# A message-passing layer and a mixture of experts on one core: the gather of pair j+2 ahead of the scatter of pair j-1 on GpSimd

## The chip, the core and the metric

The kernel runs on one core of one Trainium2 chip. The metric is the device time of one execution in microseconds (us); a program on one core has the time of that core. Before the change, three runs took 1000.0, 990.54 and 1000.09 us, with a median of 1000.0.

## What is computed

The input is 1250 rows of 512 floats and 20000 edges. Two layers follow each other, each added to its input:

```python
x = x + gnn(layernorm(x), edge_index, edge_type, edge_weight, ...)   # attention over edges, then a layer norm
x = x + ffn(layernorm(x), ...)                                        # 64 experts, two per row, and a shared one

# ffn, for T = 1250 rows, E = 64 experts, D = 512, H = 256
scores = sigmoid(xt @ Wg.T + bg)
w, idx = top_k(scores, 2);  w = w / w.sum(-1)
nx = layernorm(xt)
h = silu((gamma[e] * nx + beta[e]) @ W1[e] + b1[e]) * (... @ W3[e] + b3[e])   # per expert e
y = sum over the two experts of w * (h @ W2[e]) + cw @ b2
z = shared expert on nx (Ws1, Ws3, Ws2)
return y + z
```

All is float32. W1 and W3 are 512 x 256 for each expert and W2 is 256 x 512, so two experts have 2 MB of W1 and W3 and 1 MB of W2.

## The kernel before

The edge layer comes first and takes until about 490 us; then come its layer norm, the router and the table of slots, and from about 597 us the experts. The change touches the experts only.

**Pairs of experts.** The experts are taken in 32 pairs (`NPAIR`), pair j being experts 2j and 2j+1, each with up to 64 rows (`TS`). `slot_tab` holds, for each pair, the 128 row numbers to read (column 0) and the 128 places to write (column 1); places that no row fills carry a number out of bounds and are skipped. What does not fit into 64 rows goes through a loop behind the pairs, which ran once here.

**The steps of one pair, by line.** All buffers between these steps have two copies, taken by j % 2.
- GpSimd gathers 128 rows of `nx_rows` (DRAM) into `xg` (line 538), which raises `xg_landed[j % 2]`.
- TensorE turns `xg` by four transposes (`turn`, lines 982 to 985, recorded as L762) and raises `pe_xgT`; VectorE scales the result (lines 1514 and 1515) and raises `xgT_done`.
- TensorE multiplies by W1 and W3 (`up`, the bias as L989, the rest as L993; raises `pe_up`). ScalarE takes the silu (L718), VectorE multiplies (L1522) and raises `hm_done`.
- TensorE turns the hidden rows (`hidden_turn`, again L762); VectorE copies them (L1525) and raises `hT_done`.
- TensorE multiplies by W2 (`down`, L1006; raises `pe_y`). ScalarE copies the 128 rows to `yo` (L721) and raises `y_ready`.
- GpSimd scatters `yo` into `y_rows` in DRAM (L543), which raises `y_out[j % 2]`.

**Order on TensorE** (lines 1013 to 1046): in iteration j it does up(j), then waits for the gather of pair j+1 (line 1022) and does turn(j+1), then down(j-1), then work on the side, then hidden_turn(j). The work on the side is the shared expert and the turned router weights in iterations 0 to 6 (`BESIDE`, L927 and L933) and one product of the biases in each of iterations 7 to 16 (L1041).

**Order on GpSimd** (lines 550 to 557): the gathers of pairs 0 and 1 ahead of the loop; then in iteration j it waits for turn(j), gathers pair j+2, waits for the output rows of pair j and scatters them. GpSimd takes its instructions one by one, so a wait holds all that stand behind it. Pair 32 is the first item of the loop behind the pairs.

**Loads of the weights.** There are three buffers (`WB`). SP issues W1 and W3 of pair j+3 when up(j) is done (lines 397 to 399, L372). ScalarE issues W2 of pair j+2 after down(j-1) (line 734, L714), but behind a wait for an earlier scatter:

```python
act.wait_ge(s("pe_y"), j)
if j >= 3:
    act.wait_ge(y_out[(j - 1) % 2], 16 * ((j - 1) // 2))   # the scatter of pair j-3 has landed
if j - 1 + WB < NPAIR:
    load_down(j - 1 + WB)
out_rows((j - 1) % 2, P, "y_ready")
```

Of the kernel before, what the change touches and what calls it, by code (L numbers as in the profile page):

```python
# [38 lines left out]
def gnn_moe_kernel(nc, x, src, dst, etype, eweight, W, a_src, a_dst, et_emb, ln_gamma, ln_beta,  # L39
# [23 lines left out]
    REST = NE - FULLC * P  # L63

    NEX, _, HF = W1.shape
    M = HF // P
    TS = TOKENS
    NOV = (2 * N) // TS
    NPAIR = NEX // 2
# [23 lines left out]
    with ExitStack() as ctx:  # L93
# [4 lines left out]
        def sem(name):  # L98
            return ctx.enter_context(nc.semaphore(name))
# [190 lines left out]
        def s(name):  # L290

            if name not in names:
                names[name] = sem(name)
            return names[name]
# [4 lines left out]
        y_out = [sem(f"y_out{k}") for k in range(2)]  # L299
# [126 lines left out]
        def _(pool):  # L426
# [110 lines left out]
            def gather(u, at, sems):  # L537
                pool.indirect_dma_start(out=xg[:, u, :], out_offset=None, in_=nx_d[:, :],
                                        in_offset=bass.IndirectOffsetOnAxis(ap=at, axis=0),
                                        bounds_check=NPAD - 1, oob_is_err=False).then_inc(sems, 16)  # L540

            def scatter(u, at, sems):
                pool.indirect_dma_start(out=y_d[:, :], out_offset=bass.IndirectOffsetOnAxis(ap=at, axis=0),  # L543
                                        in_=yo[:, u, :], in_offset=None, bounds_check=2 * NPAD - 1,
                                        oob_is_err=False).then_inc(sems, 16)

            def slots(j, k):
                return slot_tab[:, j:j + 1, k:k + 1].rearrange("p a b -> p (a b)").bitcast(U32)

            gather(0, slots(0, 0), xg_landed[0])  # L550
            gather(1, slots(1, 0), xg_landed[1])
            for j in range(NPAIR):
                if j + 2 <= NPAIR:
                    pool.wait_ge(s("pe_xgT"), j + 1)
                    gather(j % 2, slots(j + 2, 0), xg_landed[j % 2])
                pool.wait_ge(s("y_ready"), j + 1)
                scatter(j % 2, slots(j, 1), y_out[j % 2])
            pool.wait_ge(y_out[0], 16 * (NPAIR // 2))
            pool.wait_ge(y_out[1], 16 * (NPAIR // 2))
            n = pool.value_load(nover_i[0:1, 0:1], min_val=0, max_val=NOV)  # L560
# [1048 lines left out]
```

## Time and profile before

| What | Value |
|---|---|
| median of three runs | 1000.0 us (990.54 to 1000.09) |
| the profiled execution's own time | 996.03 us |
| its span, first to last instruction | 994.3 us |
| busy: TensorE, VectorE, ScalarE, GpSimd | 719.7, 546.5, 276.1, 385.8 us |
| mean granted TensorE clock | 0.836 of full speed |
| bytes moved, mean rate over the span | 190.72 MB, 192 GB/s |

The span and the rows come from one execution; the granted clock of 1.00 is 2.4 GHz and that of 0.50 is 1.2 GHz; 1.7 us of its time lie outside its span. PE is TensorE's matrix work and PEld its loading of weights into the array, which runs beside it; DVE is VectorE, ACT ScalarE, POOL GpSimd, and SPq and ACTq are the instructions by which SP and ScalarE issue transfers. "DMA share" is the mean busy share of the core's 16 DMA engines. A row of the timeline that stands for several instructions (x4) gives the time from the first one's start to the last one's end. A number in square brackets at the end of such a row is the time for which the engine sat idle before it, and what ended that.

### The profile page before, as it was taken

The page shows a single profiled execution, that of the slowest core. Times are in us where ns is not written, and L with a number is a line of the kernel's source. Part 1 is how long each engine was busy: PE and PEld are TensorE (multiplying, and loading weights), DVE is VectorE, ACT ScalarE, POOL GpSimd, SP SyncE. Part 2 cuts the span into 40 slices and gives each one's busy share as a digit, 9 for nine tenths or more (in the row PEclk, how much of TensorE's full clock was granted, in tenths as well). Part 3 has the DMA queues.
Part 4 walks back from the last instruction along what each step waited for, and adds up shares of the span by engine and source line. Part 5 has one row for each costly group of instructions (what it writes and reads, how often), then busy time and mean ns, then how long its engine had stood idle before and what let it go on. Part 6 is the DMA issues. An engine that isn't in the chain of part 4 may idle for free.

```text
span 994.3 us, 12428 instructions
## 1 busy us (share of the span) xinstructions
PE 719.7 (72%) x3500; PEld 375.2 (38%) x3500; DVE 546.5 (55%) x1238; ACT 276.1 (28%) x735; POOL 385.8 (39%) x397
## 2 busy tenths in 40 slices
PE   0979885156987797776607999898787877777740
PEld 0966563133544344443306554333232222222210
DVE  4978999844876576667897584223232221221205
ACT  0344441157254655455026310110001000010000
POOL 2415543976277777778353011112111121122110
PEclk9777988577998889978755799999999898898885
DMA  5323435376168656855132006889889788888228
GB/s 176 88 58 100 106 97 160 89 215 181 48 173 268 209 165 178 295 165 141 68 122 84 23 15 233 295 307 362 303 304 330 295 309 291 309 330 299 97 76 309
DMA packets 67755, 190.72 MB, mean 192 GB/s; under 512 B 15420, under 2 KB 16625, under 8 KB 67712
## 3 DMA queue, kind: packets, MB, share of 16 engines
q1 hardware_dynamic: 37172, 99.66, 28.9%
q0 software_dynamic: 19440, 56.41, 18.7%
q10 hardware_dynamic: 11100, 34.11, 9.8%
q8 instruction: 24, 0.39, 0.2%
q14 instruction: 19, 0.16, 0.0%
HBM read 180.78 MB, written 16.57 MB: 198 GB/s over the span
## 4 chain that ended last, share of the span: by engine, by line
PE 43%; DVE 17%; DMA 16%; issue 12%; another core or an unknown queue 3%; POOL 3%; ACT 2%; DVEq 1%; ACTq 1%; POOLq 0%; SPq 0%
PE ps L877 14%; DMA xn<-nx_rows,slot_tab 12%; PE ps L1006 8%; PE ps L762 5%; DVE edge L1210 3%; PE ps L880 3%; POOL y_rows L543 3%; DVE arena L1203 2%; PE ps L927 2%; PE ps L993 2%; PE ps L821 2%; ACT xn L721 2%; DMA ring<-y_rows 2%; PE ps L841 1%
## 5 line engine op out<-in xcount | busy, mean ns | idle before, releaser
L877 PE MATMUL ps<-ring,edge 128*128 128x512 f32 x320 | 180.5, 692 | 66.5 <-DVE ring L1286 35.0
L489 POOL DMA_INDIRECT ring<-h_rows,idx_stage x160 | 171.9, 1074 | 42.9 <-issue 38.8
L635 ACT ACTIVATE ring<-ring,edge 128x64 f32<-128x64 f32 x480 | 128.6, 336 | 115.3 <-DMA ring<-h_rows,idx_stage 101.0
L543 POOL DMA_INDIRECT y_rows<-xn,slot_tab x32 | 33.5, 1047 | 280.7 <-ACT xn L721 268.2
L762 PE MATMUL ps<-ident,xn 128*128 128x128 f32 x278 | 62.9, 355 | 98.0 <-DMA xn<-nx_rows,slot_tab 60.8
L1282 DVE TENSOR_SCALAR edge<-iota_row,dloc 128x128 f32<-128x128 f32 x176 | 61.2, 348 | 89.8 <-remote 57.8
L877 PEld LDWEIGHTS ps<-ring,edge 128*128 128x128 f32 x320 | 61.9, 216 | 114.5 <-issue 64.8
L762 PEld LDWEIGHTS ps<-ident,xn 128*128 128x128 f32 x278 | 46.8, 212 | 152.8 <-DMA xn<-nx_rows,slot_tab 85.5
L1522 DVE TENSOR_TENSOR xn<-ps,xn 128x256 f32<-128x256 f32 (+1 forms) x33 | 14.0, 425 | 148.5 <-ACT xn L718 81.1
L993 PE MATMUL ps<-arena,xn 128*64 128x512 f32 x352 | 80.8, 601 | 0.0
L1006 PE MATMUL ps<-arena,xn 128*64 128x512 f32 x260 | 78.6, 727 | 0.9 <-DVE xn L1525 0.9
L1286 DVE TENSOR_TENSOR ring<-ring,edge 128x320 f32<-128x320 f32 x160 | 77.6, 485 | 0.0
L880 PEld LDWEIGHTS ps<-edge 128*128 128x128 f32 x352 | 58.2, 207 | 48.6 <-issue 48.6
L457 POOL TENSOR_SCALAR arena<-arena 24x1280 bf16<-24x1280 bf16 (+1 forms) x11 | 37.9, 3450 | 80.3 <-DMA arena<-edge_keys 80.3
L721 ACT COPY xn<-ps 128x512 f32<-128x512 f32 (+1 forms) x33 | 19.3, 585 | 164.5 <-PE ps L1006 164.5
L466 POOL TENSOR_TENSOR spare<-iota_p 128x1 f32<-128x1 f32 x63 | 21.0, 334 | 105.4 <-DVE slot_tab L1483 54.4
L1274 DVE TENSOR_TENSOR acc<-ps,acc 128x512 f32 x88 | 60.6, 688 | 0.4 <-issue 0.4
L718 ACT ACTIVATE xn<-ps 128x256 f32<-128x256 f32 (+1 forms) x33 | 12.6, 383 | 168.9 <-PE ps L993 168.9
L1210 DVE TENSOR_REDUCE edge<-arena 128x40 f32<-128x800 f32 (+1 forms) x32 | 50.4, 1576 | 4.8 <-DVE arena L1203 4.6
L880 PE MATMUL ps<-edge 128*128 (+1 forms) x352 | 47.9, 245 | 0.0
L993 PEld LDWEIGHTS ps<-arena,xn 128*64 128x64 f32 x352 | 23.4, 137 | 56.4 <-issue 56.4
L821 PE MATMUL ps<-arena,xT 128*128 128x512 f32 x80 | 43.7, 697 | 0.0
(284 smaller groups left out, 1046.5 us busy)
## 6 DMA issues: line engine op xcount, KB each, us to landing
arena<-in_L_ffn_W_dram SPq DMA_DIRECT2D x47, 1024.0 KB, 10.8
arena<-in_L_ffn_W_dram ACTq DMA_DIRECT2D x29, 1024.0 KB, 5.4
edge<-in_L_ffn_W_dram SPq DMA_DIRECT2D x20, 1024.0 KB
arena<-edge_keys SPq DMA_DIRECT2D x20, 320.0 KB
ring<-y_rows SPq DMA_DIRECT2D x9, 512.0 KB, 6.3
ring<-edge_keys SPq DMA_DIRECT2D x10, 320.0 KB
h_rows<-ring SPq DMA_DIRECT2D x10, 256.0 KB, 4.5
ring<-h_rows,idx_stage POOLq DMA_INDIRECT x160
```

Of the source, the lines that this page charges most:

```text
L489: pool.indirect_dma_start(out=(ring2 if lo == 1 else ring)[:, slot, :], out_offset=None, in_=h_d[:, :], in_offset=bass.IndirectOffsetOnAxi ...
L543: pool.indirect_dma_start(out=y_d[:, :], out_offset=bass.IndirectOffsetOnAxis(ap=at, axis=0), in_=yo[:, u, :], in_offset=None, bounds_chec ...
L635: o = act.activation(rows[:, k, h * HD:(h + 1) * HD], rows[:, k, h * HD:(h + 1) * HD], ACT.Copy, scale=p_c[:, bass.ds(SLOTS * i + k, 1), h ...
L762: return pe.transpose(o, i, ident[0:n, 0:n])
L821: o = pe.matmul(ps[:, 7, :], xT[:, a, t * P:(t + 1) * P], WT[:, a, :], start=(a == 0), stop=(a == A - 1))
L877: pe.matmul(ps[:, j % 4, :], S[:, k % 4, :], rows[:, k, :], start=(u == 0), stop=(u == 1))
L880: o = pe.matmul(ps[:, 4 + j % 4, 0:H], S[:, k % 4, :], p_c[:, bass.ds(SLOTS * i + k, 1), :].rearrange("p a h -> p (a h)"), start=(u == 0), ...
L993: o = pe.matmul(ps[c, 2 + k, :], xgT[:, k, a, c], w13[b][:, x, :, a, :], start=False, stop=(a == A - 1), skip_group_check=True)
L1006: o = pe.matmul(ps[c, 5 + k, :], hT[:, k, m, c], w2s[b][:, x, m, :], start=(m == 0), stop=(m == M - 1))
L1210: link(v.tensor_reduce(e_c[:, c0:c0 + n, :], prod[:, 0:n * 2 * NT * H].rearrange("p (c k h) -> p c h k", c=n, h=H), AX_X, ALU.add))
L1282: v.tensor_scalar(S[:, k % 4, :], iota_row[:, :], dloc[:, bass.ds(SLOTS * i + k, 1)], None, ALU.is_equal)
L1286: v.tensor_tensor(rows[:, k, 0:n].rearrange("p (h d) -> p h d", d=HD), rows[:, k, 0:n].rearrange("p (h d) -> p h d", d=HD), p_c[:, bass.ds ...
```

## The change

The loop on GpSimd gets one more iteration, and in iteration j the scatter is that of pair j-1 instead of pair j. The gather keeps its place at the head of the iteration and its wait.

```diff
-            for j in range(NPAIR):
+            for j in range(NPAIR + 1):
                 if j + 2 <= NPAIR:
                     pool.wait_ge(s("pe_xgT"), j + 1)
                     gather(j % 2, slots(j + 2, 0), xg_landed[j % 2])
-                pool.wait_ge(s("y_ready"), j + 1)
-                scatter(j % 2, slots(j, 1), y_out[j % 2])
+                if j >= 1:
+                    pool.wait_ge(s("y_ready"), j)
+                    scatter((j - 1) % 2, slots(j - 1, 1), y_out[(j - 1) % 2])
```

Written out, with G for a gather and S for a scatter, the queue of GpSimd was G0 G1 G2 S0 G3 S1 G4 S2 ... G32 S30 S31 and becomes G0 G1 G2 G3 S0 G4 S1 G5 S2 ... G32 S29 S30 S31. The count of instructions, their sizes and all semaphores stay the same.

## Rows read from the trace of the kernel before

**Rows 1.** The page, the chain that ended last: shares by line.
```profile
PE ps L877 14%; DMA xn<-nx_rows,slot_tab 12%; PE ps L1006 8%; PE ps L762 5%; DVE edge L1210 3%; PE ps L880 3%; POOL y_rows L543 3%; DVE arena L1203 2%; PE ps L927 2%; PE ps L993 2%; PE ps L821 2%; ACT xn L721 2%; DMA ring<-y_rows 2%; PE ps L841 1%
```
**Rows 2.** Waits, 600 to 994 us: engine, line, releaser: us, times, longest.
```profile
POOL y_rows L543 <- ACT xn L721: 268.2, 31, 18.5
...
PE ps L762 <- DMA xn<-nx_rows,slot_tab: 60.8, 25, 4.1
...
PE ps L989 <- DMA arena<-in_L_ffn_W_dram: 3.3, 1, 3.3
```
**Rows 3.** Timeline, 819 to 835 us: start, us, engine, line, operation.
```profile
821.63 0.75 PE L762 MATMUL ps<-ident,xn 128*128 128x128 f32 x4 [2.42 <-DMA xn<-nx_rows,slot_tab]
...
822.32 1.94 PE L1006 MATMUL ps<-arena,xn 128*64 128x512 f32 x8
...
824.71 0.58 ACT L721 COPY xn<-ps 128x512 f32<-128x512 f32 x1 [5.06 <-PE ps L1006]
...
825.48 3.65 PE L993 MATMUL ps<-arena,xn 128*64 128x512 f32 x16
...
826.10 1.03 POOL L543 DMA_INDIRECT y_rows<-xn,slot_tab  x1 [7.56 <-ACT xn L721]
...
827.43 1.01 POOL L538 DMA_INDIRECT xn<-nx_rows,slot_tab  x1 [0.30 <-issue]
...
829.17 1.01 SPq L372 DMA_DIRECT2D arena<-in_L_ffn_W_dram  x2
...
833.21 1.13 PE L762 MATMUL ps<-ident,xn 128*128 128x128 f32 x4 [4.07 <-DMA xn<-nx_rows,slot_tab]
...
834.26 3.68 PE L1006 MATMUL ps<-arena,xn 128*64 128x512 f32 x8
```
**Rows 4.** Timeline of PE alone: bias products of pairs 1, 7, 8, 31; three turns.
```profile
605.86 1.02 PE L989 MATMUL ps<-arena,xn 128*128 128x512 f32 x2
...
622.20 0.75 PE L762 MATMUL ps<-ident,xn 128*128 128x128 f32 x4 [0.87 <-DMA xn<-nx_rows,slot_tab]
...
632.44 0.75 PE L762 MATMUL ps<-ident,xn 128*128 128x128 f32 x4 [1.94 <-DMA xn<-nx_rows,slot_tab]
...
655.66 0.75 PE L762 MATMUL ps<-ident,xn 128*128 128x128 f32 x4 [1.39 <-DMA xn<-nx_rows,slot_tab]
...
672.82 1.02 PE L989 MATMUL ps<-arena,xn 128*128 128x512 f32 x2
...
681.29 1.02 PE L989 MATMUL ps<-arena,xn 128*128 128x512 f32 x2
...
938.54 1.02 PE L989 MATMUL ps<-arena,xn 128*128 128x512 f32 x2
```
**Rows 5.** Windows of 1 us, PE alone: length, busy, clock, DMA share, GB/s.
```profile
634.00:635.00 1.00, 1.00 (x6) 0.50 1.06 434
775.00:776.00 1.00, 1.00 (x8) 1.00 0.00 0
834.00:835.00 1.00, 1.00 (x4) 0.50 1.03 414
```
**Rows 6.** Longer windows: length, PE, PEld, DVE, ACT, POOL, clock, DMA share, GB/s.
```profile
680.00:690.00 10.00, 7.34 (x32) 2.88 (x32) 2.10 (x5) 0.97 (x2) 2.05 (x2) 1.00 1.01 403
...
780.00:790.00 10.00, 7.19 (x29) 2.65 (x29) 2.70 (x6) 0.44 (x2) 2.04 (x2) 0.85 1.02 404
...
870.00:880.00 10.00, 5.97 (x26) 2.33 (x24) 0.85 (x2) 0.97 (x2) 2.04 (x2) 0.95 1.00 367
```
**Rows 7.** Window 625 to 925 us, the same columns.
```profile
625.00:925.00 300.00, 241.23 (x914) 85.66 (x911) 74.09 (x149) 27.37 (x57) 55.20 (x54) 0.92 0.85 310
```
**Rows 8.** DMA, 600 to 994 us: GpSimd's queue: packets, MB, share; issues to landing.
```profile
q0 software_dynamic: 5120, 9.74, 7.0%
...
xn<-nx_rows,slot_tab POOLq DMA_INDIRECT x30, 4.5
...
y_rows<-xn,stage_s POOLq DMA_INDIRECT x1, 2.3
```
**Rows 9.** Timeline of PE: the first bias product behind the pairs.
```profile
953.73 2.08 PE L989 MATMUL ps<-arena,xn 128*128 128x512 f32 x2 [3.26 <-DMA arena<-in_L_ffn_W_dram]
```

## The prediction

> **What bounds the kernel now.** I read the chain first. Its second entry is the transfer that fetches rows for the experts, with 12% of the span [rows 1], which is 0.12 x 994.3 = 119 us and all of it behind 600 us. A chain share is not what would be saved, since it holds the whole flight of each gather, beside which TensorE partly works. So the view of waits comes next, for that stage: TensorE itself sat idle 60.8 us in 25 waits for the gather, and for weights in a single wait of 3.3 us [rows 2], which belongs to the loop behind the pairs [rows 9]. No pair waited for its weights. GpSimd meanwhile stood 268.2 us before its scatters [rows 2].
>
> The timeline shows why the gather is late [rows 3]. Turn, down, hidden turn and up run from 821.63 to 825.48 + 3.65 = 829.13 us. The output rows are copied at 824.71, the scatter goes out at 826.10, and only behind it, at 827.43, the gather for the next turn. It lands some 5 us later, so TensorE is idle for 4.07 us, until 833.21. The two buffers of `xg` had long allowed that gather: turn of the pair before ended at 822.4. What held it was the wait for the output rows, one place ahead in GpSimd's queue.
>
> DMA is close to being the bound but isn't. Over 625 to 925 us its share was 0.85 at 310 GB/s [rows 7], and there are stretches in which nothing moved at all, such as 775 to 776 us with TensorE at work [rows 5]: all that had been asked for had landed, up to two pairs ahead.
>
> **What the change does, part by part.** Nothing is added: 33 gathers ahead of the extra loop and 32 scatters remain, near 1 us of GpSimd each [rows 3]. The gather of pair j+2 used to stand behind the scatter of pair j-1, which waits for down(j-1) in TensorE's iteration j. Now it stands behind the scatter of pair j-2, so it goes out in iteration j-1. Its own wait, for turn(j), is met in the same iteration ahead of down(j-2), so it adds no wait. The pattern on GpSimd (scatter, then gather, some 2.7 us behind the copy) stays as it is; the gather in it is merely the one for a pair later. Its lead over the need grows by one pair. It was 829.13 - 827.43 = 1.7 us; it becomes 1.7 us plus a cycle of at least 7.5 us, so at least 9.2 us. The median flight is 4.5 us [rows 8], the one of rows 3 took at most 5.8. So the 60.8 us of waits go, in the present queues. The scatters move past one gather each; that gather was issued an iteration earlier, and nothing waits in front of the scatter that did not before. The cost of this move I put at 0; were its cover gone, it would be one issue, 1.0 us [rows 3], of which ScalarE would feel nothing before a scatter were two pairs late.
>
> A second thing goes with the waits. After 4.07 us of idleness the granted clock is 0.50, the lower level of 1.2 GHz [rows 5]: down takes 3.68 us instead of 1.94 and turn 1.13 instead of 0.75 [rows 3]. That is 2.1 us per such wait.
>
> **What is late next.** TensorE without the waits, from the bias product of pair 1 at 605.86 us [rows 4]: up to pair 7 it stands at 672.82 now. The waits in that stretch are 0.87, 1.94 and 1.39 us, and the second was followed by the lower clock at 634 us [rows 5], 2.1 us: sum 6.3, so pair 7 comes at 666.5. From pair 7 to 17 each cycle has the bias product on the side, 681.29 - 672.82 = 8.47 us without a wait [rows 4], so 84.7 us. The last 14 cycles are 829.13 - 821.63 = 7.5 us each [rows 3], 105 us. Pair 31 could thus start at 666.5 + 84.7 + 105 = 856.2 us, where it starts at 938.54 now [rows 4]. TensorE alone would give 82.3 us.
>
> The weights don't allow all of it. A pair has 3 MB of weights, 3.146 MB in the decimal count. GpSimd's queue moved 9.74 MB in 64 transfers [rows 8], 0.30 MB for a gather and a scatter. So a pair is 3.45 MB. At 8.47 us that would be 407 GB/s, at 7.5 us 460 GB/s, and the fullest stretches of 10 us show 403, 404 and 367 [rows 6]. The rate when DMA never rests is not in this trace for long. The bounds: 404 GB/s, 8.54 us per pair, from above; from below the 310 GB/s at share 0.85, scaled to a full share, 365 GB/s or 9.45 us. The low estimate charges for the thin parts in which a gather or scatter runs alone and which would then lie beside weights. I take 385 GB/s, between them and near the mean 391 of the three full stretches: 9.0 us.
>
> W1 and W3 of pair j+3 are issued when up(j) ends. From the end of up(7), at 666.5 + 4.7 = 671.2 us, until those of pair 31 have landed are 22 pairs, from 10 to 31. 22 x 9.0 = 198 us, which gives 869 us. That is 13 us behind TensorE's own 856, so DMA ends last and the weights take the gather's place in the waits, from about the twentieth pair, once the lead of two pairs is used up. TensorE then idles about 1.5 us per cycle; waits of 2.0 and 2.4 us in this trace kept the full clock, as the one before 821.63 did [rows 3], so I charge nothing there.
>
> Pair 31 moves from 938.5 to 869: -69.5 us. What follows it is untouched: the last down, the loop behind the pairs and the stores wait for the same things. The profiled execution took 996.0 us, which gives 926.5. The median of the runs, 1000.0, lies 4 us over the profiled one, so the sum is put at 1000.0 - 69.5 = 930.5, and I say 931.
>
> The full stretches show 403 and 404 GB/s [rows 6]. The Trainium skill's page "DMA: Bandwidth & Descriptors", section "Where 436 GB/s comes from", says that for transfers between HBM and SBUF the memory side binds at about 358 GB/s for a core. The trace disagrees over 10 us, but not over 200, and the rule is a rival below.
>
> **The rivals.**
> - *The sustained rate is lower.* The queues can't hold what 10 us of them show: 345 to 365 GB/s, the scaled rate of rows 7 being its upper end. For it speaks that 870 to 880 us gave 367 at a full share [rows 6]. Against it, two of three full stretches gave over 400. At 358 GB/s a pair is 9.64 us, 22 of them 212 us, pair 31 starts at 883: -55 us, 945. With 345 it is 10.0 us, 220, 891: -47, 953. (By the skill's rule it would be just this 358 and 945.)
> - *TensorE stays the bound.* DMA holds 404 or more, pair 31 comes at 671.2 + 22 x 8.54 = 859 us or at TensorE's 856: -80 to -82, so 918 to 920. The idle 1 us at 775 [rows 5] speaks for slack; the 460 GB/s that 7.5 us would ask speaks against.
> - *The new waits cost clock.* If each wait for weights brought the lower level, a cycle would be 2.1 us longer: 856.2 + 24 x 2.1 = 907 us, -32, 968. The falls at present follow waits near 4 us, and a slower TensorE gives DMA time, which ends the waits. Weak.
> - *The gather stays late*, because with two of them ahead and full queues it flies longer than 9 us, or because its place depends on something that I misread: within 1% of before, 990 to 1010. The longest wait now is 4.1 us, so flights are near 6.
> - *Slower: the scatters land too late.* ScalarE waits for the scatter of pair j-3 ahead of the W2 load and of the copy. In a DMA queue that never empties a write to DRAM could take long. The place: that wait; the price: a cycle becomes (flight + 2.4 us from copy to issued scatter) / 2 [rows 3]. It is now (938.54 - 672.82) / 24 = 11.07 us [rows 4]. The time rises by over 1% only where the cycle passes 11.07 + 16/24 = 11.74, so with flights over 21 us. At 24 us the cycle is 13.2, +51 - 6: 1045. The one flight shown is 2.3 us [rows 8] with empty queues, gathers fly 4.5 in half full ones; 21 is far.
>
> **How the numbers follow.** My forecast (DMA ends last at 370 to 400 GB/s, 922 to 941) has 0.55, the lower rate 0.25, TensorE as the bound 0.10, the clock 0.04, the late gather 0.03, the scatters 0.03. The first three span 917 to 953; with the spread of the runs (990.5 to 1000.1) the range is 914 to 957, which leaves out about 0.15. A measurement of this kernel tells about 1% from no change. Faster by over 1%: all but the last two, 0.94. Within 1%: 0.03. Slower: 0.03.
>
> **What would show it.** In the profile after, the wait of TensorE's L762 for the gather should be near zero; waits of L989 or L993 for the weights (arena, edge) should appear in the last third; GpSimd should issue scatter and gather in the same pattern; the share of DMA from about 680 us on should be 0.97 or more, at 370 to 400 GB/s; pair 31's bias product should come near 869 us, with the cycles of pairs 8 to 16 at 8.5 us and the last ones at 9.0. If DMA's share stays under 0.9 with no gather wait left, my account of what is late next is wrong; if the gather wait is still there, that of the queue is.

## The result, and the profile after

The changed kernel took 928.96 us in the median of four runs (921.75 to 930.88), the one before 1000.05 us in four runs (990.54 to 1001.14). The ratio is 0.9295 with a 95% interval of 0.9219 to 0.9372: 7% faster. The prediction was 931 us. Executions more than 1.5% above the fastest of their kernel are left out of the ratios here, so that a ratio need not be the quotient of the two medians, and three of the profiled executions below (the release put back, W2 issued by SP, the last of the spread kernel) are of that kind.

The profiled execution took 930.39 us with a span of 928.6 us. The diff adds one line ahead of TensorE's code, so each line there is one higher: L763 is the turns (L762 before), L990 the first bias product of a pair (L989), L994 up, L1007 down.

The waits of TensorE behind 590 us, whole, to set against [rows 2] (engine, line, releaser: us, times, longest):

```profile
engine line waited for: us in total, times, longest us
PE ps L990 <- DMA arena<-in_L_ffn_W_dram: 10.6, 6, 3.5
PE ps L990 <- DMA edge<-in_L_ffn_W_dram: 2.7, 1, 2.7
PE ps L763 <- issue: 1.9, 1, 1.9
PE ps L763 <- DVE xn L1523: 0.9, 1, 0.9
PE ps L1007 <- DVE xn L1526: 0.9, 2, 0.5
PE ps L990 <- issue: 0.6, 1, 0.6
```

The 60.8 us of waits for the gather are gone to the last one. In their place stand 13.3 us of waits for weights, 3.5 of them in the loop behind the pairs. The page of the kernel after says the same of the chain: the gather's entry of 12% [rows 1] is missing and the weights have 7%.

```profile
PE ps L878 15%; PE ps L994 10%; DMA arena<-in_L_ffn_W_dram 7%; PE ps L763 5%; PE ps L1007 5%; PE ps L881 3%; DVE edge L1211 3%; PE ps L928 3%; PE ps L990 3%; DVE arena L1204 3%; PE ps L822 2%; PE ps L934 2%; DMA ring<-y_rows 2%; PE ps L798 2%
```

Where the time went is read best from the bias products, one per pair (timeline of TensorE; pairs 0, 7, 8, 17, 18, 20, 21, 22, 25, 29, 30 and 31; compare [rows 4]):

```profile
600.47 1.10 PE L990 MATMUL ps<-arena,xn 128*128 128x512 f32 x2 [0.59 <-issue]
...
670.25 1.02 PE L990 MATMUL ps<-arena,xn 128*128 128x512 f32 x2
678.52 1.02 PE L990 MATMUL ps<-arena,xn 128*128 128x512 f32 x2
...
752.98 1.02 PE L990 MATMUL ps<-arena,xn 128*128 128x512 f32 x2
760.41 1.02 PE L990 MATMUL ps<-arena,xn 128*128 128x512 f32 x2
...
775.26 1.02 PE L990 MATMUL ps<-arena,xn 128*128 128x512 f32 x2
785.57 1.48 PE L990 MATMUL ps<-arena,xn 128*128 128x512 f32 x2 [2.72 <-DMA arena<-in_L_ffn_W_dram]
794.75 1.02 PE L990 MATMUL ps<-arena,xn 128*128 128x512 f32 x2
...
820.58 2.08 PE L990 MATMUL ps<-arena,xn 128*128 128x512 f32 x2 [2.67 <-DMA arena<-in_L_ffn_W_dram]
...
855.67 1.13 PE L990 MATMUL ps<-arena,xn 128*128 128x512 f32 x2 [2.66 <-DMA edge<-in_L_ffn_W_dram]
863.95 1.12 PE L990 MATMUL ps<-arena,xn 128*128 128x512 f32 x2 [0.59 <-DMA arena<-in_L_ffn_W_dram]
871.53 1.13 PE L990 MATMUL ps<-arena,xn 128*128 128x512 f32 x2
```

From pair 7 to 17 each cycle is 8.27 us, then 7.43 us, without a wait, until pair 21. From there weights are late for six of the ten pairs 21 to 30. I call the time from the bias product of pair 0 to that of pair 31 the stage. It is 871.53 - 600.47 = 271.1 us, and was 938.54 - 596.98 = 341.6 us: 70.5 us less. Ahead of the stage this execution was 3.5 us later than the profiled one of before, and behind it 57.1 us against 55.8.

The windows (columns as in [rows 6]):

```profile
671.00:860.00 189.00, 179.83 (x741) 63.94 (x740) 57.53 (x121) 21.36 (x44) 45.02 (x44) 0.98 1.01 402
788.00:789.00 1.00, 1.00 (x6) 0.37 (x4) 0.00 (x0) 0.00 (x0) 0.00 (x0) 0.50 1.03 414
860.00:870.00 10.00, 9.41 (x42) 3.62 (x42) 3.15 (x8) 1.35 (x3) 2.05 (x2) 1.00 0.74 281
870.00:880.00 10.00, 9.49 (x42) 3.19 (x40) 2.36 (x5) 1.56 (x3) 1.65 (x2) 1.00 0.07 25
```

DMA moved 402 GB/s over these 189 us, where it had 310 at a share of 0.85 [rows 7]. Its share was still 0.81 from 670 to 680 us and full from there on (shares a little over 1 are read as full), with 408 GB/s from 700 to 860 us. It ran dry between 860 and 880 us, when the last weights were in. The second row is the lower clock behind the wait of 2.72 us.

### The profile page after: what moved, and what is told of

Same layout as the page of the kernel before. It is cut to its first block, busy times and chain, and to the rows that moved or that the text cites. A ratio compares the mean times of both kernels' runs of the same rounds, so it can differ in the third digit from the quotient of the medians.

```text
span 928.6 us, 12428 instructions
## 1 busy us (share of the span) xinstructions
PE 701.8 (76%) x3500; PEld 373.9 (40%) x3500; DVE 544.1 (59%) x1238; ACT 276.8 (30%) x735; POOL 388.4 (42%) x397
## 4 chain that ended last, share of the span: by engine, by line
PE 55%; DVE 20%; DMA 10%; issue 8%; another core or an unknown queue 3%; ACT 1%; DVEq 1%; SPq 0%; POOLq 0%; POOL 0%
PE ps L878 15%; PE ps L994 10%; DMA arena<-in_L_ffn_W_dram 7%; PE ps L763 5%; PE ps L1007 5%; PE ps L881 3%; DVE edge L1211 3%; PE ps L928 3%; PE ps L990 3%; DVE arena L1204 3%; PE ps L822 2%; PE ps L934 2%; DMA ring<-y_rows 2%; PE ps L798 2%
## 5 line engine op out<-in xcount | busy, mean ns | idle before, releaser
L878 PE MATMUL ps<-ring,edge 128*128 128x512 f32 x320 | 178.5, 685 | 69.9 <-DVE ring L1287 41.8
L489 POOL DMA_INDIRECT ring<-h_rows,idx_stage x160 | 179.3, 1121 | 44.1 <-issue 40.3
L763 PE MATMUL ps<-ident,xn 128*128 128x128 f32 x278 | 59.8, 342 | 35.4 <-ACT xn L666 32.6
L994 PE MATMUL ps<-arena,xn 128*64 128x512 f32 x352 | 82.2, 610 | 0.0
L763 PEld LDWEIGHTS ps<-ident,xn 128*128 128x128 f32 x278 | 46.6, 215 | 83.2 <-issue 77.0
L1007 PE MATMUL ps<-arena,xn 128*64 128x512 f32 x260 | 63.9, 604 | 0.9 <-DVE xn L1526 0.9
L466 POOL TENSOR_TENSOR spare<-iota_p 128x1 f32<-128x1 f32 x63 | 16.4, 260 | 104.2 <-DVE slot_tab L1484 54.0
L990 PE MATMUL ps<-arena,xn 128*128 128x512 f32 x66 | 36.9, 643 | 13.9 <-DMA arena<-in_L_ffn_W_dram 10.6
L994 PEld LDWEIGHTS ps<-arena,xn 128*64 128x64 f32 x352 | 23.8, 140 | 56.9 <-issue 56.9
```

The source lines that it names most:

```text
L489: pool.indirect_dma_start(out=(ring2 if lo == 1 else ring)[:, slot, :], out_offset=None, in_=h_d[:, :], in_offset=bass.IndirectOffsetOnAxi ...
L763: return pe.transpose(o, i, ident[0:n, 0:n])
L878: pe.matmul(ps[:, j % 4, :], S[:, k % 4, :], rows[:, k, :], start=(u == 0), stop=(u == 1))
L990: pe.matmul(ps[:, 2 + k, :], sel[:, k, :], bb1[:, :], start=True, stop=False, skip_group_check=True)
L994: o = pe.matmul(ps[c, 2 + k, :], xgT[:, k, a, c], w13[b][:, x, :, a, :], start=False, stop=(a == A - 1), skip_group_check=True)
L1007: o = pe.matmul(ps[c, 5 + k, :], hT[:, k, m, c], w2s[b][:, x, m, :], start=(m == 0), stop=(m == M - 1))
```

## The experiments

The runs were made on several chips, and the part ahead of the stage differs between them: pair 0 starts at 558 to 565 us on one and at 597 to 614 us on the others. On the first of these the kernel before itself took 948 to 964 us and the intervals are wide, so there the stage decides. So I compare ratios to the kernel before on the same chip, and the stage in the profiles, which repeats: the changed kernel gave 271.1, 271.5 and 271.8 us. A flight is the time from a gather's or scatter's issue to its landing; a lead is the time from a gather's issue to the end of the up behind which TensorE needs its rows.

### The release put back

```diff
                     pool.wait_ge(s("pe_xgT"), j + 1)
+                    if j >= 1:
+                        pool.wait_ge(s("y_ready"), j)
                     gather(j % 2, slots(j + 2, 0), xg_landed[j % 2])
```

> The changed kernel with one wait added: the gather of pair j+2 goes ahead of the scatter of pair j-1, as changed, but it waits for the output rows of pair j-1 as it did before the change. So it is released as late as before and only stands one place further ahead. Theory A (the late release is the cause): the gather goes out 1.3 us earlier than before the change, its lead of 1.7 us becomes 3.0, still short of a flight near 5; 25 waits shrink by about 1.3 us each and some falls of the clock go with them: 950 to 975 us, with 20 to 40 us of TensorE's waits for the gather left. Theory B (the place behind the scatter, in GpSimd's issue and in its DMA queue, is the cause): as the changed kernel, 925 to 935 us, with no such wait left.

Measured: 933.08 us against 957.33 of the kernel before, ratio 0.9764 (0.9653 to 0.9875); stage 314.9 us. The only kind of wait that the pairs are left with (TensorE's waits of this run):

```profile
PE ps L765 <- DMA xn<-nx_rows,slot_tab: 41.1, 19, 3.8
```

The stage is 26.7 us under that of before and 43.8 over that of the change, the waits are just above the range of theory A, and so is the time, 0.9764 of 1000 us. Going 1.3 us earlier buys 38% of the gain in the stage; the release buys the rest. B falls: ahead of the scatter but released late, the gather is still late.

### The release halfway

```diff
-                    pool.wait_ge(s("pe_xgT"), j + 1)
+                    pool.wait_ge(s("pe_xgT"), j + 2)
                     gather(j % 2, slots(j + 2, 0), xg_landed[j % 2])
```

> The changed kernel, but the gather of pair j+2 waits for turn(j+1) instead of turn(j), so it is released at that turn and its lead over the need is about 6.5 us, between the 3.0 of the run with the wait kept and the 9.2 or more of the changed kernel. Theory A (only the lead against the flight counts): flights under full queues are 5 to 7 us, so waits for the gather of 0 to 10 us are left and the stage (pair 0 to 31) is 271 to 282 us against 271.1 of the changed kernel. Theory B (the order ahead of the scatter counts, not the lead): 271 us and no waits; this alone does not part from A, but a stage of over 290 us would speak against both.

Measured: ratio 0.9417 (0.9313 to 0.952), stage 279.7 us. The views of the gather's line and of the timeline of this run:

```profile
  PE ps L763: 18.4, 18
...
DMA to landing us min/median/max: 2.1/7.2/7.8
```

```profile
796.47 1.01 POOL L538 DMA_INDIRECT xn<-nx_rows,slot_tab  x1 [3.45 <-PE ps L763]
...
804.15 0.75 PE L763 MATMUL ps<-ident,xn 128*128 128x128 f32 x4 [1.70 <-DMA xn<-nx_rows,slot_tab]
```

The stage fits; the waits, 18.4 us, do not: I had put 0 to 10. Flights had grown to a median of 7.2 us, over the 5 to 7 of the expectation, because DMA now never rests (387 GB/s at a share of 1.00 from 680 to 860 us). With a lead of 6 us there is thus still a small wait in many pairs. Not all of it costs time: the stage is 8.6 us longer than that of the changed kernel, because the 9.8 us of waits for weights among the pairs are gone in exchange.

Together with the kernels before and after, these are four leads and four sums of waits: 1.7 us, 60.8; 3.0 us, 41.1; 6 us, 18.4; 9.1 us and more, none. Each lead is that of the last pairs, from about 20 on. Where TensorE has a bias product beside, in pairs 9 to 18, it is longer: 2.5 us before the change, 6.8 us here and 10.8 us in the changed kernel. One gather of the changed kernel and the turn that needs it, near its shortest lead (timeline):

```profile
797.67 1.01 POOL L538 DMA_INDIRECT xn<-nx_rows,slot_tab  x1 [0.31 <-issue]
...
806.72 0.75 PE L763 MATMUL ps<-ident,xn 128*128 128x128 f32 x4
```

### Bytes taken from the changed kernel

```diff
 # ScalarE's load of W2
-act.dma_start(w2s[j % WB].rearrange("p x m d -> p x (m d)"), W2[...].rearrange("o (p m) d -> p o (m d)", m=M))
+act.dma_start(w2s[j % WB][:, :, 0, :], W2[...].rearrange("o (p m) d -> p o m d", m=M)[:, :, 0, :])
```

> The changed kernel with half of W2 left out of the loads of pairs 3 to 31 (0.52 MB less per pair; the products use what lies there). Theory A (behind the change DMA ends last, from about pair 21): the waits for weights, 13.3 us, go, and with them the falls of the clock behind the three long ones, some 5 us; pair 31 starts near 857 us instead of 871.5, and the time falls by 12 to 17 us, to 912 to 917. Theory C (TensorE is the bound and the waits for weights take up time that is free anyway): 927 to 930 us.

Measured: ratio 0.9156 (0.9051 to 0.9261); stage 256.5 us, which is 14.6 under the changed kernel, as A had it. 0.9156 of 1000 us is 916, in the range of A; in absolute terms it was 872.13 us, on the chip with the short part ahead. There is no wait for weights among the pairs, and TensorE is busy without a gap, 256.5 of the 256.5 us of the stage; a part of it (window of this run):

```profile
640.00:800.00 160.00, 160.00 (x680) 57.52 (x676) 53.57 (x113) 19.77 (x41) 41.09 (x41) 1.00 0.99 372
```

So 256.5 us is TensorE's own time for the stage at 2.4 GHz, and the changed kernel is 14.6 us above it because of bytes. C falls.

### Bytes taken from the kernel before

The same edit on the kernel before the change.

> The kernel before the change with the same half of W2 left out. Theory A (it is bound by the chain of output rows, scatter, gather and turn, and bytes matter only through the flight of the gather): 980 to 997 us, with most of the 60.8 us of waits for the gather still there. Theory D (bytes were the bound already and the wait for the gather merely took the place of one for weights): 29 x 0.52 MB at 310 GB/s is 49 us less, 945 to 960 us.

Measured: ratio 0.9656 (0.9502 to 0.981), that is 33 us of 957; stage 311.7 us, 29.9 less.

```profile
PE ps L762 <- DMA xn<-nx_rows,slot_tab: 42.8, 25, 6.5
```

Between the two theories, and a larger gain than A allowed. No pair waits for weights, so bytes were not the bound; but they count for more than I gave them, through the flight. Its median is 3.5 us here and 4.2 in the kernel before. A second run, of two executions, went further along the same line, with a quarter of W1 and W3 and half of W2 loaded from pair 3 on:

```diff
-                    sp.dma_start(w13[j % WB][:, :, w, :, :]..., wt[...].rearrange("o (p a) h -> p o (a h)", a=A))
+                    # from pair 3 on
+                    sp.dma_start(w13[j % WB][:, :, w, 0, :], wt[...].rearrange("o (p a) h -> p o a h", a=A)[:, :, 0, :])
```

> The kernel before the change with two thirds of the bytes of the weights left out from pair 3 on (a quarter of W1 and W3 and half of W2 are loaded, 1.05 MB per pair instead of 3.15). The gather stays where it was, released by the output rows of the pair before. Theory A (the wait for the gather is its lead of 1.7 us set against a flight that the weights in the queues make long): the flight falls toward the 2.1 us of the one gather that flew alone, waits for the gather to under 20 us, and the stage (pair 0 to 31) from 341.6 to 257 to 280 us. Theory A1 (the flight is the gather's own and the queues matter little): waits of 40 us and more, and a stage over 300 us.

Measured: stage 292.6 us, ratio 0.9581 (0.9511 to 0.9651). From the view of the gather's line in this run: TensorE's waits for it (us, times) and its flights:

```profile
  PE ps L767: 29.7, 24
...
DMA to landing us min/median/max: 2.1/3.2/4.3
```

Again between the theories. DMA's share is 0.46 at 146 GB/s (680 to 860 us), and still the gather flies 3.2 us in the median and TensorE waits at 24 of its 31 turns. The share fell less than the bytes did; the quarter of W1 and W3 comes in runs of 1 KB where the whole comes in runs of 4 KB, which may be why, but this was not tried by itself. So the weights in the queues are half of the story: they lengthen the flight and double the waits, from 29.7 to 60.8 us. The other half is the lead: the 1.7 us of the last pairs are too little for any flight, the shortest being 2.1 us, and the 2.5 us of pairs 9 to 18 are too little for the median one.

### The loads moved away from the gather

```diff
                 sp.wait_ge(s("pe_up"), j - WB + 1)
+                sp.wait_ge(s("pe_xgT"), j - WB + 2)
                 load_up(j)
```

> The kernel before the change, but SP issues the W1 and W3 loads of a pair only when the turn behind the up that frees their buffer is done, so these 2 MB are no longer put into the queues while the gather flies. All bytes stay. Stage means the time from the bias product of pair 0 to that of pair 31; it was 341.6 us before the change. Theory A2 (the flight of the gather is long because those loads go out beside it): flights fall from near 5 us to 3 or 4, the waits for the gather from 60.8 to 20 to 40 us, and the stage to 300 to 325 us. Theory A1 (the flight is that of the gather itself): waits near 60 us and the stage within 5 us of 341.6. Against both stands a new cost, DMA resting a few us per pair; if weights then come late, L989 waits for arena or edge.

Measured: 1038.57 us, ratio 1.0365 (1.0275 to 1.0454); stage 372.6 us. This went the wrong way, by 31 us. From the view of the gather's line (TensorE's waits and the flights), then the timeline and windows of this run around one gather:

```profile
  PE ps L763: 87.2, 29
...
DMA to landing us min/median/max: 2.1/5.3/7.5
```

```profile
853.36 0.90 SPq L372 DMA_DIRECT2D edge<-in_L_ffn_W_dram  x2
...
859.26 1.01 POOL L539 DMA_INDIRECT xn<-nx_rows,slot_tab  x1 [0.30 <-issue]
...
864.63 0.75 PE L763 MATMUL ps<-ident,xn 128*128 128x128 f32 x4 [3.67 <-DMA xn<-nx_rows,slot_tab]
```

```profile
862.00:863.00 1.00, 0.00 (x0) 0.00 (x0) 0.00 (x0) 0.00 (x0) 0.00 (x0) 1.00 0.98 387
863.00:864.00 1.00, 0.00 (x0) 0.00 (x0) 0.00 (x0) 0.00 (x0) 0.00 (x0) 1.00 0.74 289
864.00:865.00 1.00, 0.37 (x3) 0.38 (x4) 0.00 (x0) 0.00 (x0) 0.00 (x0) 1.00 0.01 4
```

Theory A2 had looked only at the load that is issued behind the gather. The 2 MB that are held back until the turn (853.36) are still being moved, with the 1 MB of W2 behind them, when the next gather goes out at 859.26, and that gather is in only as the queues run dry, at 864. In the kernel before, those 2 MB went out at the end of up, 8 us or more ahead of the next gather (819.26 and 827.43 us in its timeline), here it is 5.9 us. The reading that fits is that all counts that the engines have in hand while the gather flies, whether it was issued before or behind it; it rests on this gather and on the shorter flights of the two runs with fewer bytes, and was not tested apart. A1 falls too: the waits are not near 60 us.

### The work on the side spread

```diff
-    BESIDE = {0: (("up", 4),), 1: (("up", 5),), 2: (("cw", 0), ("cw", 1)), 3: (("cw", 2), ("down", 3)),
-              4: (("down", 4), ("down", 5)), 5: (("down", 6), ("down", 7)), 6: (("down", 8), ("down", 9))}
+    BESIDE = {0: (("up", 4),), 2: (("up", 5),), 4: (("cw", 0), ("cw", 1)), 5: (("cw", 2), ("down", 3)),
+              7: (("down", 4),), 9: (("down", 5),), 11: (("down", 6),), 13: (("down", 7),), 15: (("down", 8),), 17: (("down", 9),)}
-    Z0 = 7
+    Z0 = 18
```

> The changed kernel with TensorE's work on the side spread: shared expert and router weights in iterations 0 to 17 instead of 0 to 6, the bias products in 18 to 27 instead of 7 to 16. The same work in all. Theory A (DMA ends last and rests while TensorE is held by side work in the first pairs, some 10 us of it from 600 to 680 us): DMA fills earlier, the waits for weights shrink to under 5 us, 917 to 923 us. Theory C (TensorE is the bound): its work is the same, 927 to 930 us.

Measured: ratio 0.9238 (0.9147 to 0.9329), stage 263.6 us, 7.5 under the changed kernel; waits of the pairs for weights 4.3 us. The chip was the one with the short part ahead (881.92 us against 957.33 of the kernel before); 0.9238 of 1000 us is 924, a little over the range of A, and the interval, 915 to 933, holds both theories. The stage decides for A: TensorE's work in it is the same, and it is shorter. DMA fills earlier: in the 65 us from some 10 us behind pair 0 it has a share of 0.96 where the changed kernel has 0.87 (windows of the spread kernel, then of the changed one).

```profile
575.00:640.00 65.00, 65.00 (x286) 25.88 (x282) 23.70 (x50) 8.85 (x19) 14.80 (x14) 1.00 0.96 376
```

```profile
611.00:676.00 65.00, 65.00 (x268) 26.63 (x266) 23.85 (x49) 7.90 (x17) 12.79 (x12) 1.00 0.87 328
```

The same edit, with the W2 loads moved to SP behind W1 and W3, so that all weights are in one queue in the order of need:

```diff
                 load_up(j)
+                sp.wait_ge(s("pe_y"), j - WB + 1)
+                load_down(j)
```

The two lines by which ScalarE issued these loads are taken out, so a scatter that has not landed no longer holds a load of W2.

> The changed kernel with the work on the side spread, as in the run of that name, and with the W2 loads issued by SP behind W1 and W3, so that all weights come in one queue in the order of need. Bytes as before. Theory A (W2 takes half the rate while both queues are full, though W1 and W3 are needed first): the waits for weights fall from 7.6 us to under 3, and the stage from 263.6 to 258 to 262 us, TensorE's own work being 256.5. Theory C (the order inside the full queues does not matter, only the bytes do): 263 to 265 us, the waits as they were.

Measured: stage 264.7 us, ratio 0.9205 (0.9085 to 0.9326), waits of the pairs for weights 5.2 us, where the two queues had 4.3. That is theory C: for this order the bytes count, not the queue in which they stand.

Then the changed kernel and the spread one on one chip, six executions each, beside the kernel before (999.73 us in 11):

> The changed kernel again, for the comparison with the spread one on one chip: stage 271 to 272 us, ratio to the kernel before the change 0.925 to 0.94.

> The changed kernel with the work on the side spread, again, beside the changed kernel on one chip: stage 263 to 265 us, so 6 to 8 us or 0.7% under the changed kernel in the same call. If the gain of the earlier run is only that of its chip, the stage is 271 us.

Measured: the changed kernel 935.85 us, ratio 0.9328 (0.9281 to 0.9374), stage 271.8. The spread one 930.13 us, ratio 0.9204 (0.9146 to 0.9263), stage 263.9. The stages of the spread kernel repeat to 0.3 us, and 263.9 against 271.8 is a gain of 7.9 us in the stage. In the whole time it is less sure. The medians of all six executions differ by 5.7 us or 0.6%, and the single ones overlap: 929.98 to 939.52 us for the changed kernel, 917.55 to 941.92 for the spread one. The two intervals of the ratios do not touch, but that of the spread kernel rests on three executions. An earlier run of the changed kernel, on the chip of the halfway run:

> The changed kernel itself, for a comparison on the chip of the other runs. Stage (pair 0 to 31) 271 us as before, within 1.5 us; its ratio to the kernel before the change between 0.925 and 0.935.

Measured: ratio 0.9358 (0.9274 to 0.9441), just above my range, and stage 271.5.

## Why the prediction was right

**The queue.** The gather goes out a pair earlier, nothing is added, and all its waits go. The halfway and the put-back release show that the lead is what does it. The lead of at least 9.2 us (9.1 measured) was enough. The profile of the changed kernel gives no landings for its gathers beside the weights, but it does for its scatters, which go through the same queue (the view of their line):

```profile
DMA to landing us min/median/max: 2.3/6.8/7.8
```

The gathers of the halfway run have the same maximum. Here the prediction was right with less room than it counted: it set 9.2 us against present flights of 4.5 and at most 5.8 us, which leaves 3.4 us, while under full queues 1.3 us are left. The rival of the late gather was thus not far off: with 6 us of lead it was there. The lead of 1.7 us was also read from the last pairs and taken for all; in pairs 9 to 18 it was 2.5 us.

**The waits' price.** 60.8 us of waits and 2.1 us per fall of the clock. Before, the stage was 341.6 - 256.5 = 85.1 us above TensorE's own time. 60.8 are waits. Set cycle by cycle against the changed kernel with half of W2, 21.9 of the other 24.3 us lie in the cycles with the ten falls of the clock, 1.6 to 3.4 us for each fall, and the rest are small gaps; so 2.1 us was a fair price. What the prediction said of when the clock falls was not. It had the falls follow waits near 4 us and waits of 2.0 and 2.4 us keep the clock. Six falls follow waits of 3.87 to 4.07 us, but four follow shorter ones: 1.94 us (its own row at 632.44 us), 2.46, 2.81 and 2.99.

**Pair 7 and TensorE's own time.** Pair 7 was put at 666.5. It came at 670.25 in an execution that was 3.5 us later at pair 0, so at 666.8. The cycles were 8.27 and 7.43 us instead of 8.47 and 7.5, since those I had read had small gaps in them; 3 us over the stage.

**What is late next.** DMA, first at pair 21 ("about the twentieth"), and halving W2 shows it: 14.6 us, where the prediction's sum had 13 (869 against 856). That pair 31 came at 871.5, or 868.0 on the start of before, against 869 is partly luck, however. Two slips of like size stand against each other. For the second, the queue of W1 and W3 in the kernel after, from 864 to 872 us and from 868 to 871 (packets, MB, share of the 16 engines):

```profile
q1 hardware_dynamic: 111, 0.41, 12.6%
...
q1 hardware_dynamic: 18, 0.06, 5.1%
```

- The rate was taken as 385 GB/s, 9.0 us per pair. It was 402 over 189 us: 76.0 MB, 22.0 pairs of 3.45 MB, 8.6 us each, so 189 us and not 198, and the sum would have ended at 671.2 + 189 = 860 us. The low estimate of 365 GB/s was thus too low.
- The sum took the 16 engines as one stream that ends all at once. They don't end together. At 864 us 0.4 MB of W1 and W3 were still to come, and from 868 us on they moved at a share of 0.05, about that of one engine of 16; the last packet ended at about 870.8 us. Pair 31 came 0.7 us behind it, at 871.53, and in the two repeats it waited for its weights itself, 0.56 and 0.73 us. So the last weights were 7 us later than the rate alone gives (867.3 on the start of before, against 860). Also, the waits are not 1.5 us in each cycle but near 2.7 us at pairs 21, 25 and 29 and under 0.7 at 24, 28 and 30. I had charged no clock for them, by the reading set right above. Behind 785.57 the bias product takes 1.48 us instead of 1.02 and up 4.94 instead of 3.65, at a granted clock of 0.50, and the next pair comes 9.18 us later instead of 7.43. The eleven cycles from pair 20 to pair 31 are 14.5 us above 7.43 each, where 9.8 us are waits: 4.7 us of clock and gaps, 3.4 of them behind the two falls.

**The rivals.** The lower sustained rate fell: not 345 to 365 but 402. By the rule of the Trainium skill's page "DMA: Bandwidth & Descriptors" in "Where 436 GB/s comes from", near 358 GB/s for a core, it would have been 945 us; this trace, of a program on one core, has 402 over 189 us. TensorE as the bound fell: it alone would have had pair 31 at 597.0 + 256.5 = 853.5, and the last W1 and W3 were in at 867.3 on the start of before. At the rate alone, 860, only 7 us would have lain between the two instead of 13, so it was nearer than my 0.10 said. The new waits did cost clock, but 3.4 us in all and not 2.1 in every cycle. The scatters that land too late: 7.8 us at most, far from 21.

**Same things behind pair 31.** 57.1 us against 55.8; over all kernels measured here it is 55.5 to 57.1, so the 1.3 us are the spread of executions.

## What to carry to other kernels

Where one in-order queue carries both the input of a later item and the output of an earlier one, look at what the output waits for: it sets when the input goes out. Release the input by what frees its buffer, and size its lead by the flight under the load that will be there afterwards (7 to 8 us here), not by today's (4.5).
When a wait goes, work out the bytes per item at the new pace. If they exceed what the fullest stretches of the trace move, DMA ends last, and then work that holds the compute engine should be spread so that DMA never rests early: here that gave another 7.5 us of the stage with the same work, though only 0.6% between the medians of the whole time.

## What was not expected of the hardware

- DMA moved 402 GB/s over 189 us, and 397 to 411 in each window of 10 us from 680 to 860 us, with two queues of weights and one of gathers and scatters at once.
- A gather of some 0.15 MB flew 2.1 us alone, 3.2 at a share of 0.46, 4.2 to 4.5 at 0.85 and 7.2 at 1.00. The mean share alone does not set it: in the run with delayed loads the flight was 5.3 us at a share of 0.74 (640 to 950 us), and there one gather landed as the queues ran dry, though it has few bytes. By which rule the engines share themselves among the queues was not tried and stays open.
- The engines of one queue do not end together. The last of W1 and W3 came some 7 us behind what the mean rate gives, the end of it at the share of about one engine of 16 (868 to 871 us). Which engine lags, and why, was not looked into.
- The length of a wait does not settle by itself whether TensorE's clock falls. In the kernel after, the waits of 2.72 and 2.67 us were followed by 1.2 GHz, the one of 2.66 us ahead of 855.67 was not. In the kernel before, a wait of 1.94 us was (634 us, [rows 5]), and one of 3.00 us was not: the turn behind it, at 709.52, takes the 0.75 us of the full clock.
- Why the waits for weights come in every fourth pair rather than in each is open too. In the spread kernel one queue or two made little difference to their sum (5.2 and 4.3 us).
